# Two edits in a convolution-attention kernel on one core: who forms and reads the attention-score products, and who adds the attention output

## What is computed

```python
# layer 0: scores between images, in the frequency domain in this kernel
scores = jnp.einsum('bntk,bnsk->bnts', qf, kf) / (np.float32(np.sqrt(Hs * Ws)) * temperature)
p_attn = jax.nn.softmax(scores, axis=-1)
av = jnp.einsum('bnts,bnsk->bntk', p_attn, vf)
...
x = x + _L0_conv_ref(_gn(x), ...)
# layer 1
t = _to_tokens(x)
t = t + _L1_attn_ref(_ln_t(t), L1_attn_Wq, L1_attn_Wk, L1_attn_Wv)
t = t + _L1_ffn_ref(_ln_t(t), ...)
```

## Time and profile before

| | |
|---|---|
| median of 3 runs | 2064.22 us (2062.46 to 2067.7) |
| the profiled execution: its own time / its span | 2063.2 us / 2061.3 us |
| TensorE busy | 1729.3 us (84%) |
| VectorE busy | 1569.2 us (76%) |
| ScalarE busy | 1059.8 us (51%) |
| GpSimd busy | 491.8 us (24%) |
| score products on VectorE (L1037), start and length | 124.25 us, 66.14 us |
| slots of the attention of layer 1 | about 870 to 1820 us of the span |

### The profile page before, as it was taken

The page is one execution under the profiler, slowest core; times in us unless marked ns, Lnnn a source line. Parts: engine busy times, 40 slices in busy tenths (PEclk is TensorE's granted clock), DMA queues, the critical chain, the costliest instruction groups (busy, mean ns, idle before and its releaser), DMA issues.

```text
span 2061.3 us, 31131 instructions
## 1 busy us (share of the span) xinstructions
PE 1729.3 (84%) x11530; PEld 1076.7 (52%) x11530; DVE 1569.2 (76%) x3012; ACT 1059.8 (51%) x1632; POOL 491.8 (24%) x591
## 2 busy tenths in 40 slices
PE   8765777899789993189999899998999999966767
PEld 8631222699789893044444444454444544434535
DVE  5789999538766689789887888778886888578345
ACT  5396000133545246356677667776667777772110
POOL 2200666100190073524200541125200311000000
PEclk9886999999899996589999999999999999998878
DMA  6550353000000050001000110001000000030686
GB/s 171 203 148 11 85 127 76 1 1 1 1 1 1 1 170 1 3 8 24 11 1 1 21 21 1 1 1 32 11 1 1 1 1 1 1 123 1 216 306 172
DMA packets 113683, 101.00 MB, mean 49 GB/s; under 512 B 39168, under 2 KB 91776, under 8 KB 112992
## 3 DMA queue, kind: packets, MB, share of 16 engines
q1 hardware_dynamic: 113536, 99.02, 17.0%
HBM read 80.27 MB, written 12.44 MB: 45 GB/s over the span
## 4 chain that ended last, share of the span: by engine, by line
PE 62%; DVE 23%; issue 6%; ACT 3%; DMA 3%; POOL 2%; SPq 1%; POOLq 0%; DVEq 0%; ACTq 0%
PE PS L451 5%; PE PS L453 5%; PE PS L452 5%; PE PS L470 5%; PE PS L472 5%; PE PS L471 5%; PE PS L1269 4%; DVE U L981 4%; PE PS L1278 4%; PE PS L433 4%; DVE U L1037 3%; PE PS L1196 3%; PE PS L1402 3%; DMA V<-in_L_ffn_weight 3%; DVE ST L1773 2%
## 5 line engine op out<-in xcount | busy, mean ns | idle before, releaser
L827 DVE TENSOR_TENSOR DB<-Z 128x1024 f16<-128x1024 f32 (+2 forms) x288 | 335.2, 1164 | 117.6 <-ACT Z L657 69.0
L654 ACT ACTIVATE Z<-PS,MI 128x1024 f32<-128x1024 f32 (+2 forms) x288 | 300.5, 1043 | 240.8 <-PE PS L453 206.8
L807 DVE TENSOR_REDUCE MI<-PS 128x1 f32<-128x512 f32 (+2 forms) x576 | 357.5, 639 | 47.7 <-PE PS L433 31.3
L657 ACT ACTIVATE Z<-PS,MI 128x1024 f16<-128x1024 f32 (+2 forms) x288 | 298.7, 1037 | 0.0
L622 POOL TENSOR_SCALAR Z<-Z,MI 128x128 f32<-128x128 f32 x128 | 89.1, 707 | 699.6 <-DVE MI L839 699.6
L981 DVE TENSOR_TENSOR U<-A,PS 128x1408 f32<-128x1408 f32 x108 | 166.1, 1615 | 1.2 <-PE PS L1368 1.2
L993 POOL TENSOR_TENSOR U<-A,U 128x1408 f32<-128x1408 f32 x36 | 113.9, 3196 | 192.0 <-DVE MI L1734 137.7
L1374 PE MATMUL PS<-U 128*32 128x352 f32 x1152 | 110.7, 480 | 0.1
L470 PE MATMUL PS<-Z,A 128*128 128x512 f16 (+3 forms) x288 | 104.0, 361 | 4.3 <-ACT CST L665 4.0
L470 PE MATMUL PS<-Z,V 128*128 128x512 f16 (+3 forms) x288 | 104.0, 361 | 3.8 <-ACT CST L665 3.6
L1269 PE MATMUL PS<-CST,A 128*66 128x128 f32 x768 | 104.8, 281 | 0.5 <-DVE A L1769 0.5
(11 more groups left out here) (412 smaller groups left out, 3710.2 us busy)
## 6 DMA issues: line engine op xcount, KB each, us to landing
V<-in_L_ffn_weight SPq DMA_DIRECT2D x32, 1024.0 KB, 7.6
A<-x_planes SPq DMA_DIRECT2D x24, 528.0 KB, 9.7
U<-in_x SPq DMA_DIRECT2D x16, 512.0 KB, 3.8
V<-in_x SPq DMA_DIRECT2D x4, 2048.0 KB, 13.9
Z<-in_x SPq DMA_DIRECT2D x16, 512.0 KB, 3.9
out<-U SPq DMA_DIRECT2D x16, 512.0 KB, 5.0
U<-e_planes SPq DMA_DIRECT2D x48, 132.0 KB, 7.2
x_planes<-Z SPq DMA_DIRECT2D x2, 1056.0 KB, 8.0
```

Source lines behind the costliest of these rows:

```text
L654: act.activation(EX32[u % 2][:, 0:w], s, ACT.Exp, scale=SCALE / (QUP * KUP), bias=pb).then_inc(sem("ex_ev"), 1)
L657: act.activation(EHI[u % 3][:, 0:w], s, ACT.Exp, scale=SCALE / (QUP * KUP), bias=pb).then_inc(sem("hi_ev"), 1)
L807: dve.tensor_reduce(bm[:, g % 2, t, k:k + 1], PS[:, 4 + chunk_no[c] % 2, 0:w], AX.X, ALU.max).then_inc(sem("ch_ev"), 1)
L827: dve.tensor_tensor(ELO[u % 3][:, 0:w], EX32[u % 2][:, 0:w], EHI[u % 3][:, 0:w], ALU.subtract).then_inc(sem("lo_ev"), 1)
```

## The change

**Scores.** VectorE keeps the operands 0 and 1 of each piece (20 of the 30 products), and reads the turned modes straight from `PS` instead of `XLT`. The third operand, the sum of real and imaginary part, is now made by TensorE as two accumulating matmuls for each piece, in banks 5 and 2, behind the turns; VectorE copies these five pieces too, since the matmuls still read `XLT`. Operand 2 of each piece (10 products) is formed by GpSimd from `XLT` into two buffers in `Z`. The Gram blocks are copied behind the products; the third product of VectorE waits for the Gram matrix, since it writes where its operand lay.

**Output of the attention.** ScalarE's copy and GpSimd's part are gone. VectorE takes the reciprocal from bank 7, and scales and adds each of the two tiles in one instruction that reads bank 7 and `U`; the second raises `os_ev`, which frees bank 7 and which the statistics wait for.

```diff
@@ -209,6 +209,13 @@
         ZP = [Uf[:, o:o + 2048].rearrange("p (n s) -> p n s", n=16) for o in (0, 2048, 5376, 7424)]
+        ZPP = [Z[:, i, 0:2048].rearrange("p (n s) -> p n s", n=16) for i in range(2)]
+        def turned(c, k, w):
+            b, o = divmod(NLC * c + k if c < 2 else 12 + k, 4)
+            return PS[0:w, (3, 4, 7, 5, 2)[b], 128 * o:128 * o + 128]
         SD = Uf[:, 12928:13952].rearrange("p (n s) -> p n s", n=NH)
@@ -611,26 +618,11 @@
-            def add_out(job):
-                _, b, g, h = job
-                n = kind_no[job]
-                pool.wait_ge(sem("os_ev"), n + 1)
-                pool.wait_ge(sem("rd_ready"), n + 1)
-                x = OTM[n % 2][:, :, 0:128]
-                for j in range(2):
-                    ins = pool.tensor_scalar(x[:, j], x[:, j], rd[:, n % 2, j:j + 1], None, ALU.mult)
-                pool_steps.later(ins)
-                u = U[:, NT * b + 4 * g + 2 * h:NT * b + 4 * g + 2 * h + 2, :]
-                pool.tensor_tensor(u, u, x, ALU.add).then_inc(sem("or_ready"), 1)
             for s in slots:
...
                             normalize(b, c)
-                if s in jobs and jobs[s][0] == "out":
-                    add_out(jobs[s])
@@ -682,12 +674,6 @@
                                        ACT.Copy).then_inc(sem("ml_ev"), 1)
-                    else:
-                        n = kind_no[job]
-                        act.wait_ge(sem("out_mm"), n + 1)
-                        if n >= 2:
-                            act.wait_ge(sem("or_ready"), n - 1)
-                        act.activation(OTM[n % 2], PS[:, 7, :].rearrange("p (j d) -> p j d", j=2)[:, :, 0:130], ACT.Copy).then_inc(sem("os_ev"), 1)
                 for c in range(2, 8, 2):
@@ -835,13 +821,17 @@
                     n = kind_no[job]
-                    dve.wait_ge(sem("os_ev"), n + 1)
-                    dve.reciprocal(rd[:, n % 2, :], OTM[n % 2][:, :, 128]).then_inc(sem("rd_ready"), 1)
+                    dve.wait_ge(sem("out_mm"), n + 1)
+                    later(dve.reciprocal(rd[:, n % 2, :], PS[:, 7, 128:385:256]))
+                    for j in range(2):
+                        u = U[:, NT * b + 4 * x + 2 * y + j, :]
+                        ins = dve.scalar_tensor_tensor(u, PS[:, 7, 256 * j:256 * j + 128], rd[:, n % 2, j:j + 1], u, ALU.mult, ALU.add)
+                    ins.then_inc(sem("os_ev"), 1)
...
                 _, b, g, h = job
-                dve.wait_ge(sem("or_ready"), kind_no[job] + 1)
+                dve.wait_ge(sem("os_ev"), kind_no[job] + 1)
                 for n in range(NT * b + 4 * g + 2 * h, NT * b + 4 * g + 2 * h + 2):
@@ -1026,17 +1016,28 @@
-        def score_products(eng, z):
-            h, k = z // (3 * NLC), z // 3 % NLC
-            xc, wc = ((2, 0), (1, 1), (0, 2))[z % 3]
+        def score_products(dve, n):
+            i, c = divmod(n, 2)
+            h, k = divmod(i, NLC)
             w = min(128, ML - 128 * k)
-            if z >= 4:
-                eng.wait_ge(sem("s_mm"), z - 3)
-            eng.tensor_tensor(ZP[z % 4][0:w], XLT[0:w, xc, k, :].unsqueeze(1).broadcast_to([w, 16, N]),
-                              CT[0:w, wc, k, 16 * h:16 * h + 16].unsqueeze(2).broadcast_to([w, 16, N]),
+            if n >= 4:
+                dve.wait_ge(sem("s_mm"), 3 * (i - 2) + c + 1)
+            if n == 2:
+                dve.wait_ge(sem("once_mm"), ONCE["gram"])
+            dve.tensor_tensor(ZP[n % 4][0:w], turned(2 - c, k, w).unsqueeze(1).broadcast_to([w, 16, N]),
+                              CT[0:w, c, k, 16 * h:16 * h + 16].unsqueeze(2).broadcast_to([w, 16, N]),
                               ALU.mult).then_inc(sem("zp_dve"), 1)
+        def pool_score_products(pool, i):
+            h, k = divmod(i, NLC)
+            w = min(128, ML - 128 * k)
+            if i >= 2:
+                pool.wait_ge(sem("s_mm"), 3 * (i - 1))
+            pool.tensor_tensor(ZPP[i % 2][0:w], XLT[0:w, 0, k, :].unsqueeze(1).broadcast_to([w, 16, N]),
+                               CT[0:w, 2, k, 16 * h:16 * h + 16].unsqueeze(2).broadcast_to([w, 16, N]),
+                               ALU.mult).then_inc(sem("zp_pool"), 1)
@@ -1158,6 +1159,10 @@
             plane_parts(pool)
+            pool.wait_ge(sem("xlt_ev"), 1)
+            pool.wait_ge(sem("x_out"), 48)
+            for i in range(2 * NLC):
+                pool_score_products(pool, i)
             pool.wait_ge(sem("once_dve"), MADE["pbar"])
@@ -1326,9 +1331,15 @@
                     w = min(128, ML - 128 * k)
-                    mm = pe.transpose(PS[0:w, (3, 4, 7)[(5 * c + k) // 4], 128 * ((5 * c + k) % 4):128 * ((5 * c + k) % 4) + 128],
-                                      XL[:, c, 128 * k:128 * k + w], ident)
+                    mm = pe.transpose(turned(c, k, w), XL[:, c, 128 * k:128 * k + w], ident)
             mm.then_inc(sem("once_mm"), 1)
+            pe.wait_ge(sem("once_dve"), MADE["ct"])
+            pe.wait_ge(sem("xet_ev"), 9)
+            for k in range(NLC):
+                w = min(128, ML - 128 * k)
+                pe.matmul(turned(2, k, w), XL[:, 0, 128 * k:128 * k + w], ident, start=True, stop=False)
+                mm = pe.matmul(turned(2, k, w), XL[:, 1, 128 * k:128 * k + w], ident, start=False, stop=True)
+            mm.then_inc(sem("xs_mm"), 1)
             pe.wait_ge(sem("xet_ev"), 9)
@@ -1338,10 +1349,14 @@
                 w = min(128, ML - 128 * k)
-                pe.wait_ge(sem("zp_dve"), z + 1)
+                zp = ZPP[z // 3 % 2] if c == 2 else ZP[(2 * (z // 3) + c) % 4]
+                if c == 2:
+                    pe.wait_ge(sem("zp_pool"), z // 3 + 1)
+                else:
+                    pe.wait_ge(sem("zp_dve"), 2 * (z // 3) + c + 1)
                 for b in range(B):
                     s = slice(32 * b, 32 * b + 32)
-                    mm = pe.matmul(PS[s, h, :], XLT[0:w, (2, 0, 1)[c], k, s], ZP[z % 4][0:w, :, s],
+                    mm = pe.matmul(PS[s, h, :], XLT[0:w, (2, 0, 1)[c], k, s], zp[0:w, :, s],
                                    start=(k == 0 and c == 0), stop=(k == NLC - 1 and c == 2))
@@ -1692,20 +1707,16 @@
             dve.wait_ge(sem("once_mm"), ONCE["xlt"])
-            for i in range(2 * NLC):
+            for i in range(3 * NLC):
+                if i == 2 * NLC:
+                    dve.wait_ge(sem("xs_mm"), 1)
                 w = 128 if i % NLC < NLC - 1 else ML - 128 * (NLC - 1)
-                ins = dve.tensor_copy(XLT[0:w, i // NLC, i % NLC, :], PS[0:w, (3, 4, 7)[i // 4], 128 * (i % 4):128 * (i % 4) + 128])
-            later(ins)
-            for k, w in ((slice(0, NLC - 1), 128), (slice(NLC - 1, NLC), ML - 128 * (NLC - 1))):
-                ins = dve.tensor_tensor(XLT[0:w, 2, k, :], XLT[0:w, 0, k, :], XLT[0:w, 1, k, :], ALU.add)
+                ins = dve.tensor_copy(XLT[0:w, i // NLC, i % NLC, :], turned(i // NLC, i % NLC, w))
             ins.then_inc(sem("xlt_ev"), 1)
-            dve.wait_ge(sem("xlt_ev"), 1)
-            dve.wait_ge(sem("once_mm"), ONCE["gram"])
+            for n in range(4 * NLC):
+                score_products(dve, n)
             for b in range(B):
                 later(dve.tensor_copy(Gd[32 * b:32 * b + 32, :], PS[32 * b:32 * b + 32, 6, 32 * b:32 * b + 32]))
-            for z in range(6 * NLC):
-                score_products(dve, z)
```

## The result

The change took 2046.32 us (median of 4 runs, 2041.42 to 2051.10) beside 2065.96 us for the kernel before (4 runs, 2062.46 to 2068.94): a ratio of 0.9905, 95% interval 0.9876 to 0.9935, or -19.6 us. The forecast was -9.0 us and 2055.2, with a range down to 2048, so the sign was right and the size was not; the time lies in the bracket of rival (a), 2042 to 2050. The profiled execution took 2051.1 us and is the slowest of its four.

The account below looks back on a forecast made before the run. VectorE's products bound the scores, with ScalarE's loop 10.64 us behind as second chain; VectorE's queue matters in the attention. Terms -10.6 - 2.1 + 8.1 - 4.4 = -9.0 us gave 2055.2 us, range 2048 to 2062.

Parts of the forecast that it names:

- rival (a): Attention: gaps at batch borders recover in full (-9.3 us), bank 7 costs 0 to 8.1; 2042 to 2050 us, chance 0.15.
- The exponential, -10.6: Scores: with products shared, the softmax's exponential starts right behind ScalarE's loop and table load, at 185.64 instead of 196.28 us.
- Rival (d): Scores: products of VectorE and GpSimd exclude each other, exponential at 215.1 us, time +20.4 us to 2085, chance 0.04.
- The tail, -2.1: End of the attention: VectorE frees bank 7 sooner for the last job, so the last statistics end 2.1 us earlier.
- Behind the borders, -4.4: Attention, two batch borders: GpSimd normalises tokens earlier, VectorE is 2.2 us less late at each, TensorE's gaps shrink by 4.4.
- Bank 7, +8.1: Attention output: VectorE frees bank 7 0.72 us after its reciprocal starts; 16 of 43 successor jobs start late, 8.1 us summed.

Follow-up runs that it names:

- the early exponential: The change, with ScalarE's loop of 128 columns cut in three and the softmax's exponential placed after 102 columns: 2033.53 us, ratio 0.9837 to the kernel before.
- The kernel that reads from SBUF: The change, but VectorE's score products read the turned modes from XLT, so both operands lie outside the accumulator: 2067.37 us, ratio 1.0003 to the kernel before.
- the kernel with the output job first: The change, with VectorE doing an output job before the first maximum of the slot: 2048.33 us, ratio 0.9906 to the kernel before.
- fills alone: The change, plus six GpSimd fills of 384 elements on unread scratch behind each output job: 2064.48 us, ratio 1.0008 to the kernel before.
- the one with VectorE's new work and work on GpSimd: The change, plus two scalings and an addition by GpSimd on unread scratch for each output job: 2065.11 us, ratio 0.9993 to the kernel before.
- the kernel with ScalarE's copy: The change with the exponential moved ahead in ScalarE's loop, and ScalarE again copying outputs from bank 7 for VectorE: 2032.44 us, ratio 0.9852 to the kernel before.
- the kernel with four fills: The change, plus four GpSimd fills of 384 elements on unread scratch behind each output job: 2056.57 us, ratio 0.9965 to the kernel before.

## Why the prediction was wrong

**The exponential, -10.6: right.** It starts 1.3 us behind the loop as foretold. The slack was seen, and the early exponential shows it from the other side: it could start 13.5 us earlier. The inner sizes were off without harm: GpSimd's product 3.61 us and not 4.65, so that its ten ended at 163.7 and the last of VectorE's at 166.8 bounded them, 2.9 us later than worked out. Of these 1.5 are the later start of the stage, and 1.4 the ten matmuls of the sums, which took 2.5 us (117.00 to 119.49) instead of 1.1 and stand ahead of the Gram matrix; the 18 products behind it took 39.64 us, 2.20 each as assumed.

**Rival (d), the products that exclude each other: rightly put aside, and for the right reason.** The kernel that reads from SBUF is it. It took the exponential to 204.94, not to the 215.1 worked out from 46.5 + 44 us in a row, because GpSimd's products are shorter.

**The tail, -2.1: -2.4.** Right.

**Behind the borders, -4.4: this is the step that failed.** The prediction took the three gaps at each of two borders, 9.3 us in all, as the most that could come back, and that bound was about right. Then it took VectorE's new work there (3.0 us of 5.2) off the relief. Measured, the two stretches with a border fell by 9.3 us together in one pair of executions and by 10.5 in the other, so the gaps went whole, with VectorE's new work in place: it took nothing off the relief that the traces show. VectorE had been waiting for GpSimd there, 17.4 us in the attention; that the new work fits into this idle time is the reading that is left, and no run took the new work out alone.

**Bank 7, +8.1: a cost as foretold, but of 4 to 5 us.** The three stretches without a border grew by 4.7 and 3.5 us, and ScalarE's copy in VectorE's place gives 4.9 us of the same stretches back, 5.2 in all. TensorE's waits by name are 7.4 us at 12 places, 0.5 before. The two instructions take 0.61 us, not 0.49, since one takes 346 ns and not the 236 scaled from L835; that makes every place some 0.1 us dearer, so the term is too large for another reason. The prediction counted every late start of the old trace in full, though one wait can stand in for another, as the kernel with the output job first shows (bank 7 -5.8, maxima +3.0).

The net of the attention is -9.9 + 4.1 = -5.8 us (means of the two pairs), where -4.4 + 8.1 = +3.7 was forecast. Of the 9.5 us between them 5.5 are the borders' and 4.0 the bank's, and they are most of the 10.6 by which the forecast missed. Rival (a), with a chance of 0.15, is what happened, by its mechanism too: the borders recover in full, and bank 7 costs something between 0 and 8.1.

**What delays the tokens.** The kernels with work on GpSimd show that the time for which its queue is held ahead of the normalising carries the cost (15.2 us by fills alone), and that its collisions with VectorE's differences make that time longer. The rule that rival (d) rests on does not touch the scores of the change, but it was at work in the attention of the kernel before: there too the scalings ran from 597 to 1916 ns and the additions from 678 to 1738, and at the shortest values the 2.25 us a job would be 1.9. Why the cost is so steep between 1.67 and 2.5 us a job is argued only: the tokens of a border are due at a fixed slot, and a delay below the slack costs nothing.

From the kernel before (923.1, the mean of two) to the one with VectorE's new work and work on GpSimd (934.9) the attention grows by 11.8 us. Some 5 of them are the bank's, in the same stretches as with the change. The other 7 lie in the first batch and at the borders, and GpSimd's work was longer there than the old and began later, so they don't show that bank 7 or VectorE's new work costs more when GpSimd is late.

What stays open: why the clock in the feed-forward part differs from execution to execution; why 5.2 us of stage in the kernel with ScalarE's copy don't show in the ratios, and why the kernel with four fills is slower by more than its stages; and the price of VectorE's new work at a border with nothing else changed.

## What to carry to other kernels

When work leaves an engine that keeps another one waiting, don't charge the waiting engine's new work against the relief at the place where it waits: here the gaps behind the borders, 9.3 us, came back whole. And don't add up all late starts at a shared bank in an old trace: they came to 8.1 us, and 4 to 5 were paid. Cutting the stage at the same jobs in both traces told the two apart, which the sum of waits by name did not. Before making one chain faster, find what is second: the slack of ScalarE's loop, 10.6 us, was the whole gain of the scores, and moving one activation ahead of 26 others brought 13.5 us more, for the price of a split loop. And count an instruction in a queue by the time that it takes in place, not undisturbed: GpSimd's three instructions of 1.8 to 1.9 us alone took 2.5 beside VectorE, and the attention lost 17.6 us to them where fills as long as the undisturbed ones cost 5.

## What was not expected of the hardware

- GpSimd's product with two broadcast operands is cheaper per element than its product with one full operand and one broadcast (L993): 3614 ns for 2048 elements, 1.76 ns each, beside 3196 for 1408, 2.27 each.
- A scalar_tensor_tensor of VectorE on 128 elements takes 346 ns with one operand in the accumulator, and 350 with that operand in SBUF instead (the kernel with ScalarE's copy); a product of 2048 elements takes 2269 with one operand in the accumulator and, where nothing disturbs it, 2271 with none. So the accumulator costs nothing extra in either length, and the 110 ns over the value scaled from L835 belong to the short instruction. The Trainium skill, "VectorE: DVE Perf Modes", section on the TRN2 errata, gives a read of PSUM (the accumulator) 120 fixed cycles at 0.96 GHz against 58 for SBUF, an estimated 65 ns more; these rows do not agree with it.
- 384 fills of 384 elements by GpSimd, which read nothing, took 417 to 470 ns, while the scaling of 128 elements in the same place of the queue took 599 to 1656: 600 to 607 where no difference of VectorE, with both operands outside the accumulator, ran beside it.
